# First tiles normalised ahead of their stage, and a new event order with four probability tiles in the softmax attentions

## The chip, the cores and the metric

One core of a Trainium2 chip. The metric is the device time of one execution in microseconds (us).

## What is computed

The input `x` is [4, 1024, 128] float32, that is 4096 tokens in 32 tiles of 128 tokens. Four layers each do a feed-forward part, an attention and the feed-forward part again, and each of the twelve reads a layer norm (without gain) of `x` and adds to `x`:

```python
x = x + 0.5 * _L0_ffn_ref(_layernorm(x), ...)      # FP4-quantised gated FFN, 128 -> 352 -> 128
x = x + _L0_attn_ref(_layernorm(x), ...)           # causal softmax attention, 16 heads of 8, then an 8-step scan and an FFN
x = x + 0.5 * _L0_ffn_ref(_layernorm(x), ...)
x = x + 0.5 * _L1_ffn_ref(_layernorm(x), ...)      # 8 experts, top 2
x = x + _L1_attn_ref(_layernorm(x), ...)           # softmax attention, no mask
...                                                # L1 ffn; L2: experts and a shared expert, linear attention with rope
x = x + 0.5 * _L3_ffn_ref(_layernorm(x), ...)      # 128 -> 512 -> 512 -> 512 -> 128
x = x + _L3_attn_ref(_layernorm(x), ...)           # linear attention
x = x + 0.5 * _L3_ffn_ref(_layernorm(x), ...)
```

## The kernel before

`x` stays in SBUF as `g.x` [128, 32, 128]. The program is a row of stages, each one `nc.Block` with a program per engine (PE, DVE, ACT, POOL, SP); engines meet at a block's end, and the next stage's first act on SP is to clear the semaphores of the stage before (`Stage.block`). In order: `start`, `ffn0_first`, `qkv0`, `core0` (causal), `finish0`, `ffn0_second`, `moe1_first`, `qkv1`, `core1` (no mask), `project1`, `moe1_second`, `moe2_first`, `attn2`, `moe2_second`, `ffn3_first`, `attn3`, `ffn3_second`. In the profile digits are left out of names, so that both `core` stages are "core", `moe1_first` and `moe2_first` are "moe_first", `ffn0_first` and `ffn3_first` "ffn_first".

**Front of a stage.** Most stages work in eight chunks of four tiles (CT = 4). `Front` (L129) has per chunk: `statistics` (DVE: four `bn_stats`, a small memset, four `bn_aggr`), `power` (POOL: add of epsilon, power of -0.5), `normalise` (DVE: four `tensor_scalar`), `turn` (PE transposes), `copy` (ACT). Its buffers are double. A chunk's statistics are issued a chunk or two ahead inside the stage, but the first chunk's cannot start before the stage. The expert stages (`sparse_stage`, L218) do it in four groups of eight tiles (GT = 8, L541 to L557 on DVE, L326 on POOL), write `xn` into the arena and store each group to DRAM by SP (L311).

**Ends of stages.** DVE adds the result of a chunk to `g.x`: `add` at L1548 (ffn0) and L1059 (linear attention), `summed` at L906 (ffn3), and in the expert stages for each chunk c `weighted(c, 0)` (L674) and the add at L689, as the expert rows of a chunk come back by DMA (SP, L322; four chunks at once, the next when a chunk has been added).

**Softmax cores.** `core_stage` (L1988) goes through 16 rounds, one for each batch and group of four heads. All engines follow one list of events, made by `order()` from a string, the rhythm. Per round, causal / not causal: `f` (41 / 55), a first score product of 128 queries (PE, 64 rows of the array, into one of three banks `one`), whose row maximum DVE takes; `d` (4 / 5), a difference of two key halves into a bank pair of `two`, folded by ACT's Relu, which shortens the maxima; `s` (24 / 32), half a step of second scores (two products, on both row halves of the array, into one of two bank pairs `two`), of which ACT takes the exponential (L2358) into `pr`; `w` (12 / 16), one step's product with the values (eight float32 matmuls of PE, L2337) out of `pr`; `o` (2), the output's transpose. When all maxima of a round are there, `rows`, `turn` and `split` bring them into rows of the queries, by way of DRAM (SP: L2178 store, L2183 two loads, each waited for); the round's first `s` waits for that. `ahead` counts the `f` events between the first `split` and the first `s`, and this distance holds in every later round. `pr` has two buffers: the exponential of step k waits until step k-2 has been weighed, and the k-th `w` weighs step k-1.

PE pairs matmuls: `turns` (L2258) lets a matmul of one row half follow one of the other, so that the two run side by side.

## Time and profile before

| | us |
|---|---|
| median of 3 runs | 3804.12 (3800.93 to 3805.26) |
| the profiled execution | 3801.16 |
| its span | 3799.2 |
| busy in the span: PE, DVE, ACT, POOL | 3159.1, 2525.5, 1999.8, 1127.6 |
| granted clock of TensorE, mean | 0.915 |

Lengths of stages, from the first DVE operation of each to that of the next: ffn0_first 18.6 to 181.6, qkv0 to 252.5, core0 to 687.6, finish0 to 911.0, ffn0_second to 1075.6, moe1_first to 1392.4, qkv1 to 1447.2, core1 to 2098, project1 to 2115, moe1_second to 2431, moe2_first to 2763.9, attn2 to 2851.9, moe2_second to 3182.2, ffn3_first to 3454.8, attn3 to 3525.7, ffn3_second to 3799.

Busy time is the time in which an engine had an instruction under way. Matmuls overlap on PE, so that PE counts as busy also where single matmuls follow each other with gaps between their data.

### The profile page before, as it was taken

To read this page: it belongs to the slowest core of one execution; us is meant where nothing else is said; L and a number is where in the kernel's file an instruction comes from. 1 tells how busy PE (TensorE), PEld (TensorE's weight loads), DVE (VectorE), ACT (ScalarE), POOL (GpSimd) and SP (SyncE) were. 2 spreads that over 40 slices of the span, in tenths; PEclk is the share of its full clock that TensorE was granted. 3 is DMA by queue.
4 is the path that set the end of the run, shared out by engine and by line. 5 is a ranking of instruction groups with operands and counts; after the bars stand their busy time and mean duration, and the time that the engine had idled before them with its cause. 6 is when DMAs were issued, how large, how long until landed. Compare 5 with 4: busy or idle time off the path is not lost. (4 is left out here: it accounts for less than half of the span.)

```text
span 3799.2 us, 61584 instructions
## 1 busy us (share of the span) xinstructions
PE 3159.1 (83%) x20415; PEld 1964.7 (52%) x20415; DVE 2525.5 (66%) x7054; ACT 1999.8 (53%) x2981; POOL 1127.6 (30%) x1154
## 2 busy tenths in 40 slices
PE   4659999786659967999999599687777886998899
PEld 2433333343447842222222488566656774887687
DVE  8888887575974458999995644453476345665665
ACT  1248888663214446999999144322332234664464
POOL 3454550111426631101010266246432651001000
PEclk8879999997869988999999699799988998999999
DMA  1043330000021132000000411401102113000100
GB/s 55 1 136 120 124 123 14 1 1 23 1 111 41 43 93 69 28 20 28 19 20 2 163 42 43 141 25 44 60 18 76 44 41 115 1 1 1 64 9 12
DMA packets 87166, 187.17 MB, mean 49 GB/s; under 512 B 23168, under 2 KB 41408, under 8 KB 83792
## 3 DMA queue, kind: packets, MB, share of 16 engines
q1 hardware_dynamic: 60048, 117.66, 9.2%
q0 software_dynamic: 26816, 65.58, 5.6%
q8 instruction: 178, 2.92, 0.3%
q14 instruction: 124, 1.02, 0.1%
HBM read 121.23 MB, written 61.34 MB: 48 GB/s over the span
## 5 line engine op out<-in xcount | busy, mean ns | idle before, releaser
L2358 ACT ACTIVATE core_pr<-core_two 128x1024 f32<-128x1024 f32 (+3 forms) x896 | 792.9, 936 | 73.7 <-PE core_two L2325 68.6
L2394 DVE TENSOR_REDUCE core_mx<-core_one 128x1 f32<-128x512 f32 x778 | 494.9, 685 | 44.7 <-PE core_one L2277 38.4
L2337 PE MATMUL core_ps_o<-core_pr,core_vals 128*32 128x512 f32 (+3 forms) x3584 | 437.9, 561 | 1.4 <-ACT core_oT L2369 0.9
L2277 PE MATMUL core_one<-arena,queries 64*128 64x512 bf16 (+3 forms) x1472 | 385.5, 363 | 32.3 <-PEq L62 18.4
L2325 PE MATMUL core_two<-queries,arena 64*128 64x512 bf16 (+3 forms) x1792 | 360.2, 360 | 14.5 <-ACT core_pr L2358 10.1
L2277 PEld LDWEIGHTS core_one<-arena,queries 64*128 64x128 bf16 x1472 | 112.9, 94 | 313.9 <-DVE core_mx L2394 155.8
L2211 POOL COPY core_vals<-arena 128x288 f32<-128x288 f32 x32 | 14.5, 453 | 712.6 <-PE core_ps_o L2337 712.6
L2388 DVE CUSTOM_DVE_ANT_0 core_junk<-core_one,core_over 128x512 bf16<-128x512 f32 (+4 forms) x334 | 202.6, 643 | 10.5 <-PE core_one L2277 8.8
L2325 PEld LDWEIGHTS core_two<-queries,arena 64*128 64x128 bf16 x1792 | 94.8, 94 | 206.1 <-ACT core_pr L2358 147.7
L2391 DVE CUSTOM_DVE_ANT_0 core_junk<-core_one,behind 128x128 bf16<-128x128 f32 (+1 forms) x360 | 152.1, 460 | 50.0 <-PE core_one L2277 49.8
L2364 ACT ACTIVATE core_over<-core_two 128x1024 f32<-128x1024 f32 (+4 forms) x167 | 157.7, 953 | 52.3 <-PE core_two L2300 39.1
L343 POOL DMA_INDIRECT expert_out<-arena,moe_second_dest_index x142 | 139.8, 985 | 147.5 <-ACT arena L516 127.5
L343 POOL DMA_INDIRECT expert_out<-arena,moe_first_dest_index x142 | 139.6, 983 | 147.9 <-ACT arena L516 128.8
L453 PE MATMUL moe_first_bank<-arena 128*128 x1136 | 157.5, 282 | 21.7 <-ACT arena L516 12.7
L453 PE MATMUL moe_second_bank<-arena 128*128 x1136 | 158.8, 284 | 17.3 <-ACT arena L516 9.8
L453 PEld LDWEIGHTS moe_first_bank<-arena 128*128 128x128 f32 x1136 | 140.3, 194 | 30.9 <-issue 29.4
L453 PEld LDWEIGHTS moe_second_bank<-arena 128*128 128x128 f32 x1136 | 141.5, 196 | 28.0 <-issue 27.7
L2337 PEld LDWEIGHTS core_ps_o<-core_pr,core_vals 128*32 128x32 f32 x3584 | 71.1, 108 | 131.8 <-issue 120.5
L110 DVE CAST moe_second_x_hi<-moe_second_bank 128x128 fp32r<-128x128 f32 x142 | 41.3, 291 | 143.9 <-PE moe_second_bank L426 104.5
L110 DVE CAST moe_first_x_hi<-moe_first_bank 128x128 fp32r<-128x128 f32 x142 | 41.3, 291 | 136.1 <-PE moe_first_bank L426 112.2
L516 ACT ACTIVATE arena<-moe_second_bank 128x128 f32<-128x128 f32 x142 | 39.4, 277 | 158.1 <-PE moe_second_bank L453 111.9
L516 ACT ACTIVATE arena<-moe_first_bank 128x128 f32<-128x128 f32 x142 | 39.4, 277 | 157.5 <-PE moe_first_bank L453 114.5
(577 smaller groups left out, 8090.4 us busy)
## 6 DMA issues: line engine op xcount, KB each, us to landing
arena<-expert_out SPq DMA_DIRECT2D x64, 256.0 KB, 3.6
expert_rows<-arena SPq DMA_DIRECT2D x16, 512.0 KB, 12.1
core_w_raw<-in_m_up POOLq DMA_DIRECT2D x25, 256.0 KB, 3.4
m_hi<-core_w_hi POOLq DMA_DIRECT2D x25, 256.0 KB, 2.4
m_lo<-core_w_lo POOLq DMA_DIRECT2D x25, 256.0 KB, 3.0
q_parts<-qkv_parts SPq DMA_DIRECT2D x16, 384.0 KB, 2.6
k_parts<-qkv_parts SPq DMA_DIRECT2D x16, 384.0 KB, 3.4
queries<-q_parts SPq DMA_DIRECT2D x64, 96.0 KB
```

The costliest lines, as they stand in the source:

```text
L110: return v.tensor_copy(dst.bitcast(F32R), src)
L343: p.indirect_dma_start(ys, bass.IndirectOffsetOnAxis(ap=dest[:, s:s + 1], axis=0), y[:, s % YB, :], None).then_inc(s_sc[s % YB], 16)
L453: mm = pe.matmul(psY[:, 0:P], hT[:, s % 2, j * P:(j + 1) * P], w_down[:, j * P:][:, bass.ds(at[s], P)], start=(j == 0), stop=(j == 3))
L516: a.activation(y[:, s % YB, :], psY[:, 0:P], ACT.Identity).then_inc(s_y, 1)
L2277: pe.matmul(one[bank[e]][:, 0:width], q_sb[rows, hq, pair, qt * P:(qt + 1) * P], k_sb[rows, hq, pair, kc * CW:kc * CW + width], start=True ...
L2325: mm = pe.matmul(into[:, side, off:CW], k_sb[rows, hq, pair, j * P:(j + 1) * P], q_sb[rows, hq, pair, c * CW + off:(c + 1) * CW], start=no ...
L2337: mm = pe.matmul(ps_o[h * 32:(h + 1) * 32, off:CW], vals[:, hq % 2, j, h, :], pr[:, k % 2, h // 2, h % 2, off:CW], start=(j == 0), stop=(k ...
L2358: a.activation(pr[:, k % 2, i, :, off:CW], two[spot[e] % 2][:, :, off:CW], ACT.Exp, scale=HD ** -0.5).then_inc(s_wide, 1)
L2364: a.activation(over[:, nth[e] % 2, :, 0:w], two[spot[e] % 2][:, :, 0:w], ACT.Relu).then_inc(s_wide, 1)
L2388: v.tensor_tensor_reduce(junk[:, bank[e], 0:width], scores, over[:, nth["diff", n, k, 0] % 2, side, 0:width], 1.0, -3.0e38, ALU.add, ALU.m ...
L2391: v.tensor_tensor_reduce(junk[:, bank[e], 0:width], scores, g.behind[:, CW - width:CW], 1.0, -3.0e38, ALU.add, ALU.max, at).then_inc(s_rea ...
L2394: v.tensor_reduce(at, scores, AX.X, ALU.max).then_inc(s_read, 1)
```

## The change

- A class `Head`. A stage built with `ahead=n` takes, at its end, the statistics of the first n tiles of `g.x`, once these have their last value, and normalises them into one of two buffers that outlast the stage (`g.head_xn`). The next stage's `Front` (or `sparse_stage`) takes it over: for its first chunk (group) each of `statistics`, `power` and `normalise` is only an increment of the semaphore, and `turn` reads the head's tiles. Ten stages get one: ffn0_first, finish0, moe1_first, moe2_first, moe2_second, ffn3_first and attn3 by four tiles (in the order of the work: for qkv0, ffn0_second, qkv1, attn2, ffn3_first, attn3 and ffn3_second), ffn0_second, moe1_second and attn2 by eight (for moe1_first, moe2_first and moe2_second). It adds five semaphores to each of the ten stages.
- Where it is put: ffn0, before the last `add`; sparse, statistics after the add of chunk 3, normalise after that of chunk 5; ffn3, in the last chunk at j = 2 and j = 3; linear attention, statistics before the last `cut`, normalise before the last two adds; finish0, in round BATCH at i = 4 and 6. POOL's power comes last in each POOL program.
- Softmax cores: `pr` has KEPT = 4 buffers in place of 2; the k-th `w` weighs step k-2 in place of k-1 (`lag`); both rhythms are new, with the same number of each letter; `ahead` is 13 and 8 in place of 12 and 11.
- In ffn3 the buffer `hidden1` lies in the `room` of the weights.

```diff
+class Head:
+    def __init__(self, st, g, n):
+        u = g.head_turn
+        g.head_turn = 1 - u
...
+    def statistics(self, v):
+        for k in range(self.n):
+            last = v.bn_stats(self.stats[:, k, :], flat(tile_of(self.g.x, k)))
+        last.then_inc(self.s_stats, 1)
+        v.wait_ge(self.s_stats, 1)
+        v.memset(self.dummy[:], 0.0)
+        for k in range(self.n):
+            last = v.bn_aggr(self.mv[:, k, :], self.stats[:, k, :])
+        last.then_inc(self.s_mv, 1)
+    def power(self, p):
+        p.wait_ge(self.s_mv, 1)
+        p.tensor_tensor(self.ve[:, 0:self.n], self.mv[:, 0:self.n, 1], self.g.eps[:, 0:self.n], ALU.add).then_inc(self.s_ve, 1)
+        p.wait_ge(self.s_ve, 1)
+        p.tensor_tensor(self.rstd[:, 0:self.n], self.ve[:, 0:self.n], self.g.mhalf[:, 0:self.n], ALU.pow).then_inc(self.s_rstd, 1)
+    def normalise(self, v):
+        v.wait_ge(self.s_rstd, 1)
+        for k in range(self.n):
+            last = v.tensor_scalar(self.xn[:, k, :], flat(tile_of(self.g.x, k)), self.mv[:, k, 0:1],
+                                   self.rstd[:, k:k + 1], ALU.subtract, ALU.mult)
+        last.then_inc(self.s_xn, 1)
...
     def statistics(self, v, c, u):
+        if c == 0 and self.head:
+            v.sem_inc(self.s_stats, 1)
+            v.sem_inc(self.s_mv, 1)
+            return
...
     def normalise(self, v, c, u, signal=True):
+        if c == 0 and self.head:
+            v.sem_inc(self.s_xn, 1)
+            return
...
@@ sparse_stage
+                if c == AT and head:
+                    v.wait_ge(s_sum, 2)
+                    head.statistics(v)
+                if c == AT + 2 and head:
+                    head.normalise(v)
@@ linear_stage
+            if head:
+                v.wait_ge(s_x, 2)
+                head.statistics(v)
             cut(last // 2)
             add(last - 2)
             divide(last - 1)
             divide(last)
+            if head:
+                head.normalise(v)
             add(last - 1)
             add(last)
@@ ffn0_stage
+            if head:
+                v.wait_ge(s_sum, 3)
+                head.statistics(v)
+                head.normalise(v)
             add(last)
@@ core_stage
-RHYTHMS = {True: (12, "fsffsfwffsfsffwsffdfsfwfsdffsfwsfsfwffsofswfdsofswfsffswsfffswfsffswffssffwffsdsffw"),
-           False: (11, "sfsfwfssffwffdfdfofsfswsfffswsfsffwsfdfffswsfffswfssffwffsfsfwffssfwfsfosfwsfffdswsfffswfsfdfsffwsff"
-                   "sfwfssffwf")}
+KEPT = 4
+RHYTHMS = {True: (13, 2, "fswffsffsfwffdsffwsfffssffssffsfwsffsfwwosffswfffdswoffsswsffwffssfwfffsdffswsfsfdf"),
+           False: (8, 2, "sfwffsfwffssfwfsffdofdfswsfffswfsfdffsfwsffsfwfssffwsfffswsfsffwfsfsfwfsffswffdffsfswsffsofdfswsfffs"
+                      "wsfsffwffs")}
-            steps_done, chunks_done = itertools.count(n * N2 - 1), itertools.count(2 * n - 1)
+            steps_done, chunks_done = itertools.count(n * N2 - lag), itertools.count(2 * n - 1)
-                    if step >= 2:
-                        a.wait_ge(s_weighed, step - 1)
-                    a.activation(pr[:, k % 2, i, :, off:CW], two[spot[e] % 2][:, :, off:CW], ACT.Exp, scale=HD ** -0.5).then_inc(s_wide, 1)
+                    if step >= KEPT:
+                        a.wait_ge(s_weighed, step + 1 - KEPT)
+                    a.activation(pr[:, step % KEPT, i, :, off:CW], two[spot[e] % 2][:, :, off:CW], ACT.Exp, scale=HD ** -0.5).then_inc(s_wide, 1)
```

## Rows read from the trace of the kernel before

**Rows 1.** Busy time in one round of each attention; columns in the first line.
```profile
core 0: us, PE busy (x) PEld busy (x) DVE busy (x) ACT busy (x) POOL busy (x), PEclk, DMA share, GB/s
...
425.24:450.64 25.40, 25.08 (x296) 9.03 (x290) 21.48 (x81) 22.36 (x32) 13.74 (x18) 1.00 0.41 129
...
1664.36:1703.04 38.68, 37.79 (x278) 9.43 (x276) 35.97 (x74) 36.59 (x40) 3.17 (x2) 1.00 0.08 23
```

**Rows 2.** Waits: ACT and DVE, a causal round, then a plain round.
```profile
ACT core_pr L2358 <- PE core_two L2325: 2.8, 8, 0.7
...
DVE core_junk L2391 <- PE core_one L2277: 3.0, 5, 1.0
...
ACT core_pr L2358 <- PE core_two L2325: 1.5, 6, 0.5
...
DVE core_mx L2394 <- PE core_one L2277: 2.1, 5, 0.7
```

**Rows 3.** Timeline (start, us, engine, line, operation): start of moe1_first.
```profile
1074.61 0.69 DVE L1551 SCALAR_TENSOR_TENSOR x<-ffn_second_ps_d,x 128x512 f32<-128x512 f32 x1 [9.20 <-PE ffn_second_ps_d L1654]
...
1075.62 1.64 DVE L544 BATCH_NORM_STATS2 moe_first_ln_stats<-x 128x6 f32<-128x128 f32 x8 [0.32 <-PEq L62]
...
1080.06 2.11 DVE L554 TENSOR_SCALAR arena<-x,moe_first_ln_mv,moe_first_ln_rstd 128x128 f32<-128x128 f32 x8
...
1085.46 1.11 PE L362 MATMUL moe_first_bank<-ident,arena 128*128 128x128 f32 x4 [0.52 <-DVE arena L554]
```

**Rows 4.** Timeline at the starts of qkv0, qkv1 and attn2.
```profile
185.48 0.87 DVE L1762 BATCH_NORM_STATS2 qkv_again_stats<-qkv_ln_xn 128x6 f32<-128x128 f32 x4
...
1398.47 1.12 PE L180 MATMUL qkv_ln_psT<-ident,qkv_ln_xn 128*128 128x128 f32 x4 [1.09 <-DVE qkv_ln_xn L170]
...
2769.65 2.05 PE L1124 MATMUL attn_ps_q<-attn_ln_xT,arena 128*128 128x512 f32 x2 [0.78 <-ACT attn_ln_xT L185]
```

**Rows 5.** ffn3_second: weight DMA's issue and landing (last column), first product.
```profile
3528.46 0.43 SPq L740 DMA_DIRECT2D ffn_second_f_w_lo<-f_lo  x1
...
ffn_second_f_w_lo<-f_lo SPq DMA_DIRECT2D x1, 256.0 KB, 4.8
...
3534.41 0.78 PE L121 MATMUL ffn_second_pair<-ffn_second_x_hi,ffn_second_f_w_hi 128*128 128x512 f32 x1
```

**Rows 6.** Timeline of DVE in the tail of moe1_second.
```profile
2424.70 1.14 DVE L678 SCALAR_TENSOR_TENSOR x<-arena,moe_second_weight,x 128x128 f32<-128x128 f32 x4 [0.64 <-DMA arena<-expert_out]
```

**Rows 7.** POOL's power beside a DVE operation, ffn0_second.
```profile
919.12 1.19 POOL L164 TENSOR_TENSOR ffn_second_ln_rstd<-ffn_second_ln_ve,minus_half 128x4 f32<-128x4 f32 x1
...
919.48 0.69 DVE L1348 SCALAR_TENSOR_TENSOR ffn_second_zq_v<-ffn_second_zq_v,ffn_second_zq_magic 128x512 f32<-128x512 f32 x1
```

**Rows 8.** Timeline of PE in a plain round.
```profile
1674.05 0.38 PE L2277 MATMUL core_one<-arena,queries 64*128 64x512 bf16 x2
...
1674.48 0.38 PE L2277 MATMUL core_one<-arena,queries 64*128 64x512 bf16 x1
...
1674.79 1.07 PE L2337 MATMUL core_ps_o<-core_pr,core_vals 128*32 128x512 f32 x8
```

**Rows 9.** Timeline of PE: value products of the causal attention, alone and adjacent.
```profile
437.76 0.64 PE L2337 MATMUL core_ps_o<-core_pr,core_vals 128*32 128x256 f32 x8
...
439.81 0.43 PE L2337 MATMUL core_ps_o<-core_pr,core_vals 128*32 128x128 f32 x8
...
684.55 1.01 PE L2337 MATMUL core_ps_o<-core_pr,core_vals 128*32 128x256 f32 x16
```

**Rows 10.** SP's DMA issues in a plain round, and landing of L2178, whole run.
```profile
1669.20 0.32 SPq L2178 DMA_DIRECT2D maxima<-core_nm  x1
...
1670.66 1.48 SPq L2183 DMA_DIRECT2D queries<-maxima  x2
...
1676.67 2.28 SPq L1800 DMA_DIRECT2D queries<-q_parts  x6
...
DMA to landing us min/median/max: 1.4/1.5/3.1
```

More of the change, by code:

```diff
@@ L160, in power @@
     def power(self, p, c, u):
+        if isinstance(c, int) and c == 0 and self.head:
+            p.sem_inc(self.s_ve, 1)
+            p.sem_inc(self.s_rstd, 1)
+            return
         p.wait_ge(self.s_mv, c + 1)
@@ L179, in turn @@
         for k in range(CT):
-            last = pe.transpose(self.psT[:, k * P:(k + 1) * P], (source or self.xn)[:, u, k, :], self.g.ident[:])
+            last = pe.transpose(self.psT[:, k * P:(k + 1) * P], (source[:, u] if source else self.tiles(c))[:, k, :], self.g.ident[:])
         last.then_inc(self.s_turned, 1)
@@ L351, in _ @@
                 scatter(s)
-                for ahead in itertools.islice(rest, min(MORE, max(0, s + R + 1 - min(FIRST + MORE * s, s + R)))):
-                    gather(ahead)
+                for n in itertools.islice(rest, min(MORE, max(0, s + R + 1 - min(FIRST + MORE * s, s + R)))):
+                    gather(n)
+            if head:
+                head.power(p)
         @block.tensor
@@ L705, in ffn3_stage @@
     f = Front(st, g)
+    head = Head(st, g, ahead) if ahead else None
     s = st.sb("silu", [P, 2, CW])
@@ L757, in _ @@
             over_chunks(p, body)
+            if head:
+                head.power(p)
         @block.tensor
@@ L916, in body @@
                         hidden(c + 1, j)
+                    if j == 2 and last and head:
+                        v.wait_ge(s_summed, 2)
+                        head.statistics(v)
+                    if j == 3 and last and head:
+                        head.normalise(v)
                     if j == 1 and c:
@@ L1115, in _ @@
                     f.power(p, c + 2, u)
+            if head:
+                head.power(p)
         @block.tensor
@@ L1509, in normalise @@
                     return
+                if c == 0 and f.head:
+                    v.sem_inc(f.s_xn, 1)
+                    return
                 v.wait_ge(f.s_rstd, c + 1)
@@ L1588, in _ @@
                 h_inverses(c + 1)
+            if head:
+                v.wait_ge(s_sum, 3)
+                head.statistics(v)
+                head.normalise(v)
             add(last)
@@ L1628, in _ @@
                 x_divide(c + 4)
+            if head:
+                head.power(p)
         @block.tensor
@@ L1884, in once @@
                     return
-                v.wait_ge(f.s_rstd, c + 1)
-                if c >= 2:
-                    v.wait_ge(f.s_xn, c - 1)
-                for k in range(CT):
-                    end = v.tensor_scalar(f.xn[:, u, k, :], flat(tile_of(g.x, c * CT + k)), f.mv[:, u, k, 0:1],
-                                          f.rstd[:, u, k:k + 1], ALU.subtract, ALU.mult)
-                end.then_inc(s_once, 1)
-                v.wait_ge(s_once, c + 1)
-                again.statistics(v, [f.xn[:, u, k, :] for k in range(CT)], c, u)
+                if c == 0 and f.head:
+                    v.sem_inc(s_once, 1)
+                else:
+                    v.wait_ge(f.s_rstd, c + 1)
+                    if c >= 2:
+                        v.wait_ge(f.s_xn, c - 1)
+                    for k in range(CT):
+                        end = v.tensor_scalar(f.xn[:, u, k, :], flat(tile_of(g.x, c * CT + k)), f.mv[:, u, k, 0:1],
+                                              f.rstd[:, u, k:k + 1], ALU.subtract, ALU.mult)
+                    end.then_inc(s_once, 1)
+                    v.wait_ge(s_once, c + 1)
+                again.statistics(v, [f.tiles(c)[:, k, :] for k in range(CT)], c, u)
             def twice(c):
@@ L1898, in twice @@
                     v.wait_ge(f.s_turned, c + 1)
-                    again.apply(v, [f.xn[:, u, k, :] for k in range(CT)], [xn2[:, u, k, :] for k in range(CT)], c, u).then_inc(f.s_xn, 1)
+                    again.apply(v, [f.tiles(c)[:, k, :] for k in range(CT)], [xn2[:, u, k, :] for k in range(CT)], c, u).then_inc(f.s_xn, 1)
             statistics(0)
@@ L2089, in put_out @@
                 products += 1
-        ahead, rhythm = RHYTHMS[causal]
+        ahead, lag, rhythm = RHYTHMS[causal]
         while ("split", 0, 0, 0) not in events:
@@ L2115, in order @@
                 normalise()
-        weigh(N * N2 - 1)
+        for step in range(N * N2 - lag, N * N2):
+            weigh(step)
         put_out(2 * N - 1)
@@ L2544, in finish0_stage @@
     rounds = range(-1, BATCH + 2)
+    head = Head(st, g, ahead) if ahead else None
     with st.block() as block:
@@ L2558, in _ @@
                         n1.power(p, at(b + 1, a) - 1, a)
+            if head:
+                head.power(p)
         @block.tensor
@@ L2831, in _ @@
                         hidden(b - 1)
+                    if b == BATCH and i == 4 and head:
+                        v.wait_ge(s_x, 2)
+                        head.statistics(v)
+                    if b == BATCH and i == 6 and head:
+                        head.normalise(v)
                     if i == 3 and ahead:
```

84 lines of the change are left out of this document (61 added, 23 removed).

## Prediction

> **What bounds the kernel now.** I read the stage table first: the two softmax cores are 435 and 651 us of 3799, and fifteen other stages share the rest, so a change at stage borders acts ten times by a little, a change of a round 32 times. Next, one round of each core in the windows view [rows 1]. A causal round takes 25.40 us and PE is busy for 25.08 of it; a plain round takes 38.68, with PE 37.79, ACT 36.59 and DVE 35.97. The reader is to see that PE is the bound in the causal rounds, and that in the plain ones all three are close. The waits view says the same from the other side [rows 2]: ACT waits 2.8 us for PE in a causal round and 1.5 in a plain one, DVE 3.0 and 2.1. Nobody is seen to wait for the probability buffers themselves. Last, the timelines at the borders. In an expert stage's front DVE needs 4.4 us from the stage's start (1075.62) until it can normalise the first group (1080.06), and PE gets the second group at 1085.46 after a short wait for DVE [rows 3]: DVE's chain sets the front's pace.
>
> **Borders, the gain.** No work is added or taken away: statistics, power and normalising of the first tiles move ahead of the border.
> Eight tiles for an expert stage: removed from its front are 1.64 us of statistics with about 0.6 of aggregation, and 2.11 of normalising [rows 3], 4.35 together. New order on DVE: statistics of groups 1 and 2 (2 x 2.24 = 4.5), then half of normalise(1), 1.05, so that PE gets the second group 5.6 us after the start where it was 9.84 (1085.46 less 1075.62): 4.2 us, three times, 12.6.
> Four tiles, from the same kinds of rows at half size (statistics 1.2, normalising 1.1, and the wait for POOL between). qkv0 starts its second norm at 185.48, 3.8 us in [rows 4]; with the head only statistics(1) stand before it, 1.2: 2.6. ffn0_second does the same work behind a memset: 2.5. qkv1's second transpose, which PE has before its first product, starts at 1398.47, 6.1 us in, and waits for DVE [rows 4]; now two statistics, power already under way, and normalise(1): 3.9, gain 2.2. In attn2 the first product starts 5.75 us in (2769.65) [rows 4]; statistics, power and normalising leave its chain, some 3.7, of which ACT's table load at the start keeps about 0.2: 3.5, and the same in attn3. In the ffn3 stages the front would gain 3, but the first product also waits for four weight loads. The last is issued at 3528.46 and lands 4.8 us later, 3533.3, and the product starts at 3534.41 [rows 5]: at most 1.1 to gain; SP has five more semaphores to clear before it issues, so 1.0 in ffn3_second, and in ffn3_first, where SP starts later still, 0.3. Four-tile heads: 2.6 + 2.5 + 2.2 + 3.5 + 3.5 + 1.0 + 0.3 = 15.6. Gross 28.2.
>
> **Borders, the cost.** In ffn0 DVE idles 9.20 us before the last add [rows 3]; eight tiles need 2.24 + 1.9 on POOL + 2.11 = 6.3, and the add queued behind does not feel it. Without that idle stretch it would cost all of it. finish0, ffn3_first and attn3 have DVE idle in the same way: 0. attn2's eight-tile normalise is 2.1 against a gap of some 1.9: 0.2. The tails of the expert stages have no such gap. DVE waits there for returning rows only for moments (0.64 us before chunk 5) [rows 6], no DMA is held up (all loads are released before the head's first instruction), and DVE works through the chunks one after the other. Eight tiles: 2.24 less 0.64, then 2.11, less what later waits absorb: 3.3 (moe1_second). Four tiles: 1.2 + 1.1 = 2.3, less these waits: 0.3 to 1.5 at each of three borders, 3.0 in all. Cost 6.5, net gain **21.7**. Bounds: 12 if the tails pay everything and the ffn3 stages gain nothing, 26 if the tails pay half.
>
> At the tails POOL's power runs beside DVE adds with two SBUF inputs. The row shows a power of 1.19 us (919.12) and such an operation at 919.48 inside it, which takes 0.69, its usual time [rows 7]; so I charge nothing. The Trainium skill says otherwise (SBUF — State Buffer, "SBUF: two separate sides"): the port pair shared by VectorE and GpSimd is an exclusive lock held for a whole instruction. By that rule each of five tails would hold DVE for up to a power, 1.2 to 1.9 us, some 6 in all, and the net gain would be 15.
>
> **Causal core.** PE is the bound, so what counts is PE's time per round. PE pairs matmuls of opposite row halves: the pair at 1674.05 takes 0.38, as long as the single one at 1674.48 [rows 8]; a single one between pairs wastes about 0.11. Between `w`, `o` and `w` I count half slots (f 1, s 2, d 4): an odd number wastes one. Before: 7 odd stretches of 14. After: 5 of 14, so 0.2 less. Each switch to a `w` also costs: after the single f at 1674.48 it starts 0.31 later, not 0.22 [rows 8], and a `w` has its own tail; two adjacent ones of 256 and 128 columns take 1.01 where 0.64 and 0.43 are 1.07 [rows 9]. So a `w` next to a `w` or `o` saves some 0.15. The new causal rhythm has three such places, made possible by the deeper `pr`; the old had none: 0.45. Together 0.65, taken as 0.7 with some gain from fewer waits, in 15.5 rounds: **10.9**. Bounds per round: -2.8, when ACT waits for nothing any more [rows 2]; +0.7, one of ACT's longest waits more, since a run of six `s` without `w` now stands in the round.
>
> **Plain core.** The same count gives 15 odd stretches after, 13 before, +0.2, and no adjacent `w`. At its `w` events the new order is mostly as far from the exponential it needs as the old one (two `s` before, and two now). Four buffers relieve a wait that the trace does not show. What is left is order alone: half a microsecond of shorter waits less 0.2, I take 0.25 per round, **3.9** in all. Bounds: -2.1, DVE's waits for PE gone [rows 2]; +0.9, the odd stretches and one long wait.
>
> The smaller `ahead` shortens the lead of the maxima's way through DRAM: the first load is issued at 1670.66 after a store at 1669.20; 1.48 for two issues and 1.4 to land give 1673.5, while SP sees the old round's last `s` done at 1676.67 [rows 10], 3.1 us of spare. Three `f` fewer take 3/55 of 38.68, 2.1. So 1.0 stays and costs nothing. The end of each core gets one more `w` behind the last exponentials, up to 0.5 each, set against an earlier start of core1's `s`.
>
> **Sum.** 21.7 + 10.9 + 3.9 = 36.5 off the profiled execution's 3801.2: 3764.7. The median of the runs is 2.9 above that execution: **3768**.
>
> **Rivals.**
> - Rhythms worth nothing (0.20): PE's pairing is lost to semaphore timing. Against it: the counts. 3804.1 - 21.7 = 3782.
> - Rhythms worth much (0.13): the orders remove half of the waits, 1.4 and 1.0 per round, 37 us, and the heads 21.7: 3745. For it: waits of 2 to 3 us per round on two engines; against it: PE's busy time leaves 0.3 and 0.9.
> - Heads absorbed (0.06): the first product of a stage has another wait behind the removed one, as in ffn3. Then the borders give 7 and the rhythms 10: 3787.
> - Slower (0.05): the maxima's way decides in the plain core. If each of its two legs takes 3.1 us, the longest landing seen [rows 10], in place of 1.4, the spare of 1.0 becomes a wait of 2.4 in 15 rounds, 36 us; with the heads' gain and nothing from the causal core, 3818. It decides from a lead of less than a microsecond on.
>
> **Numbers.** The forecast case has 0.56 with its own range 3756 to 3780. The range for 8 in 10 is 3744 to 3790: it leaves out the slower case, half of the absorbed one and the far ends of the second and third. A measurement can tell 0.2%, 7.6 us. Faster by more: 0.56 + 0.20 + 0.13, and 0.03 of the absorbed case, 0.92; slower by more: 0.04; within: 0.04.
>
> **What the profile would show.** Period of the causal rounds 24.7 us (25.40), of the plain ones 38.4 (38.68). In an expert front the second group's transposes 5.6 us after the stage's first DVE operation; ffn0's last add with about 3 us idle before it; the tail of moe1_second longer by 3.3. It is wrong if the plain period rises, if PE's first `s` of a round waits for "queries<-maxima", if DVE operations in the tails stretch beside POOL's power, or if fronts start early and the end of the stage does not move.

## The result

The changed kernel takes 3758.9 us (median of 4, 3755.9 to 3762.5) against 3802.5 for the kernel before, timed beside it; the ratio on record is 0.9898 (0.9886 to 0.9909), 35 to 43 us faster, where the two medians by themselves are 43.6 us apart (0.9885), just outside that interval. The forecast was 3768 with a range of 3744 to 3790. The profiled execution took 3759.6 us, its span is 3757.8.

The page of the changed kernel, its span and part 1:

```profile
span 3757.8 us, 61674 instructions
## 1 busy us (share of the span) xinstructions
PE 3150.6 (84%) x20415; PEld 1975.6 (53%) x20415; DVE 2525.3 (67%) x7057; ACT 1992.2 (53%) x2981; POOL 1128.5 (30%) x1154
```

DVE, ACT and POOL do the same work as before, to within 8 us of busy time; PE is busy for 8.5 us less. All of the change is in when things are done.

**One round of each core**, the windows view of the changed kernel, answering to [rows 1]:

```profile
core 0: us, PE busy (x) PEld busy (x) DVE busy (x) ACT busy (x) POOL busy (x), PEclk, DMA share, GB/s
469.38:493.97 24.59, 24.33 (x293) 9.50 (x293) 22.42 (x82) 22.11 (x31) 13.77 (x18) 1.00 0.43 133
1753.73:1791.73 38.00, 37.77 (x280) 9.76 (x278) 35.49 (x73) 36.33 (x40) 3.17 (x2) 1.00 0.09 24
```

A causal round fell from 25.40 to 24.57 us in most rounds (24.48 in the last four), a plain one from 38.68 to 38.00, to a hundredth the same in 14 rounds. Over 15 rounds that is 12.5 and 10.2 us. The waits view of the same rounds, answering to [rows 2] (total us, times, longest):

```profile
ACT core_pr L2473 <- PE core_two L2440: 1.8, 4, 0.7
...
DVE core_junk L2506 <- PE core_one L2392: 1.7, 5, 0.7
...
ACT core_pr L2473 <- PE core_two L2440: 0.9, 4, 0.3
...
DVE core_junk L2503 <- PE core_one L2392: 1.3, 2, 0.8
DVE core_mx L2509 <- PE core_one L2392: 0.6, 2, 0.4
```

The first two are the causal round's, where they were 2.8 and 3.0; the others the plain round's, where ACT's was 1.5 and DVE's 2.1, which is 1.9 in two lines now. All but the last fell clearly, but in a round whose length is set by PE they would fall anyway when PE gets quicker. What came first is not in this view.

**DVE beside POOL.** DVE is busy for 22.42 us of the causal round where it was 21.48. Nearly all of the difference is one small cast, by which the maxima's `split` makes a bf16 part. The timeline of POOL and DVE in the round above, and of DVE in a later one:

```profile
472.62 1.27 POOL L2341 TENSOR_TENSOR core_w_lo<-core_w_raw,core_w_hi 128x512 fp32r<-128x512 f32 x1
472.84 1.13 DVE L2522 CAST core_nm<-core_left 32x128 bf16<-32x128 f32 x1
...
571.12 0.21 DVE L2522 CAST core_nm<-core_left 32x128 bf16<-32x128 f32 x1
```

In the eight rounds in which POOL's operation (part of its work on weights) starts just before the cast, the cast takes 1.11 to 1.13 us and ends 0.08 us behind POOL's; in others it takes 0.21. In steady rounds of the old order the two don't meet, and it takes 0.21 throughout. The new order put it where POOL is at work. When POOL's work on the weights is over, in the last four rounds, the period is 24.48 us, and the step that has become shorter is an `f` that waits for DVE behind the `split`: this costs some 0.09 us a round.

**A front and a tail.** The timeline (start, us, engine, line, operation) from the end of ffn0_second into moe1_first, answering to [rows 3]:

```profile
1048.03 1.63 DVE L147 BATCH_NORM_STATS2 ffn_second_head_stats<-x 128x6 f32<-128x128 f32 x8
...
1052.37 2.14 DVE L164 TENSOR_SCALAR head_xn<-x,head_mv,head_rstd 128x128 f32<-128x128 f32 x8 [2.03 <-POOL head_rstd L159]
...
1057.15 0.69 DVE L1655 SCALAR_TENSOR_TENSOR x<-ffn_second_ps_d,x 128x512 f32<-128x512 f32 x1 [2.64 <-PE ffn_second_ps_d L1764]
1058.35 1.65 DVE L620 BATCH_NORM_STATS2 moe_first_ln_stats<-x 128x6 f32<-128x128 f32 x8 [0.50 <-PEq L62]
...
1060.22 1.07 PE L434 MATMUL moe_first_bank<-ident,head_xn 128*128 128x128 f32 x8 [3.11 <-DVEq L629]
...
1063.93 1.12 PE L434 MATMUL moe_first_bank<-ident,arena 128*128 128x128 f32 x4 [0.52 <-DVE arena L633]
```

The head of eight tiles lies whole in DVE's idle stretch: of 9.20 us ahead of the last add 2.64 are left, and the add still waits for PE. In the next stage the second group is transposed 5.58 us after the stage's first DVE operation (1063.93 less 1058.35), where it was 9.84.

The same view of DVE and POOL in the tail of moe1_second, answering to [rows 6] and [rows 7]:

```profile
2391.00 1.14 DVE L757 SCALAR_TENSOR_TENSOR x<-arena,moe_second_weight,x 128x128 f32<-128x128 f32 x4 [0.25 <-DMA arena<-expert_out]
...
2392.66 1.64 DVE L147 BATCH_NORM_STATS2 moe_second_head_stats<-x 128x6 f32<-128x128 f32 x8
...
2394.90 1.11 DVE L757 SCALAR_TENSOR_TENSOR x<-arena,moe_second_weight,x 128x128 f32<-128x128 f32 x4
2395.92 0.68 DVE L768 TENSOR_TENSOR x<-x,arena 128x512 f32<-128x512 f32 x1
2396.53 1.13 DVE L757 SCALAR_TENSOR_TENSOR x<-arena,moe_second_weight,x 128x128 f32<-128x128 f32 x4
...
2398.18 2.13 DVE L164 TENSOR_SCALAR head_xn<-x,head_mv,head_rstd 128x128 f32<-128x128 f32 x8
...
2395.35 1.67 POOL L159 TENSOR_TENSOR head_rstd<-head_ve,minus_half 128x8 f32<-128x8 f32 x1
```

Here there is no idle stretch to lie in: DVE has no wait from 2391.00 to the end, and each head operation pushes the rest back. POOL's power (2395.35 to 2397.02) runs beside 2395.92 and 2396.53, which take the usual 0.68 and 1.13.

**By stages.** The traces show each meeting of the engines at a block's end. From one to the next, in us, with the kernel of the cores alone (below) as a second measure of what a stage takes without a head. It ran on another chip, on which the expert stages are shorter (last section), so they are compared by their tails only:

| stage | before | after | cores alone |
|---|---|---|---|
| qkv0 | 70.85 | 68.66 | 71.11 |
| core0 | 435.42 | 421.18 | 424.00 |
| ffn0_second | 165.49 | 161.71 | 165.48 |
| qkv1 | 54.77 | 51.72 | 54.64 |
| core1 | 651.18 | 641.28 | 640.89 |
| moe1_second | 315.86 | 320.04 | |
| moe2_first | 332.81 | 323.45 | |
| attn2 | 88.02 | 83.32 | 86.38 |
| attn3 | 70.67 | 67.11 | 70.50 |
| ffn0_first | 163.95 | 168.56 | 165.26 |
| ffn3_second | 273.71 | 277.30 | 273.63 |

The stages left out changed by -3.1 (moe1_first) to +1.1 us (project1). The last two rows are a warning. ffn0_first came out 4.6 us longer though its head lies in a gap. Four fifths of that is there before the head: its last chunk's `hq_magic` (L1346 before, L1446 after) starts 3.60 us later. The first stage does not come near the changed lines until its last chunk. moe2_first is a warning the other way: it is 9.4 us shorter, of which its front and its tail explain 2 (4.07 gained, 2.0 paid, see below). With its head it took 329 to 336 us in the four `cut` kernels on two other chips, and of the two kernels on a third chip the one with heads took 295.2, the one without 293.7. So one profile of a stage can be off by some 4 us, and of an expert stage by 7, and the gain of the heads is not read from these rows but from the kernels below.

### The profile page after: what moved, and what is told of

Same layout as the page of the kernel before. It is cut to its first block and busy times, and to the rows that moved or that the text cites. A ratio compares the mean times of both kernels' runs of the same rounds, so it can differ in the third digit from the quotient of the medians.

```text
span 3757.8 us, 61674 instructions
## 1 busy us (share of the span) xinstructions
PE 3150.6 (84%) x20415; PEld 1975.6 (53%) x20415; DVE 2525.3 (67%) x7057; ACT 1992.2 (53%) x2981; POOL 1128.5 (30%) x1154
## 5 line engine op out<-in xcount | busy, mean ns | idle before, releaser
L2392 PE MATMUL core_one<-arena,queries 64*128 64x512 bf16 (+3 forms) x1472 | 375.8, 363 | 28.2 <-PEq L62 18.4
L2440 PE MATMUL core_two<-queries,arena 64*128 64x512 bf16 (+3 forms) x1792 | 342.4, 360 | 9.4 <-ACT core_pr L2473 6.8
L2503 DVE CUSTOM_DVE_ANT_0 core_junk<-core_one,core_over 128x512 bf16<-128x512 f32 (+4 forms) x334 | 202.2, 644 | 25.7 <-PE core_one L2392 21.0
L525 PE MATMUL moe_first_bank<-arena 128*128 x1136 | 158.0, 283 | 19.3 <-ACT arena L588 10.9
## 6 DMA issues: line engine op xcount, KB each, us to landing
expert_rows<-arena SPq DMA_DIRECT2D x13, 512.0 KB, 12.6
```

Source lines behind the costliest of these rows:

```text
L525: mm = pe.matmul(psY[:, 0:P], hT[:, s % 2, j * P:(j + 1) * P], w_down[:, j * P:][:, bass.ds(at[s], P)], start=(j == 0), stop=(j == 3))
L2392: pe.matmul(one[bank[e]][:, 0:width], q_sb[rows, hq, pair, qt * P:(qt + 1) * P], k_sb[rows, hq, pair, kc * CW:kc * CW + width], start=True ...
L2440: mm = pe.matmul(into[:, side, off:CW], k_sb[rows, hq, pair, j * P:(j + 1) * P], q_sb[rows, hq, pair, c * CW + off:(c + 1) * CW], start=no ...
L2503: v.tensor_tensor_reduce(junk[:, bank[e], 0:width], scores, over[:, nth["diff", n, k, 0] % 2, side, 0:width], 1.0, -3.0e38, ALU.add, ALU.m ...
```

## Experiments

The kernels of the first two parts up to `lag_two` ran 4 to 10 times, the others once each, so that from these only periods and positions within the profile are read. Periods are those of the rounds in steady state (from one `rows` reduction of DVE to the next), which within a run repeat to 0.02 us over most rounds (but for `new_order_lag_one`); where a chip's clock or the expert stages differ, that does not touch them: the kernel before's 25.40 and 38.67 came back on both chips.

### The parts alone

```diff
 heads_only:   KEPT = 2, old strings, lag 1, ahead 12 and 11
 cores_only:   no stage has ahead=
```

Heads only. 

> The changed kernel with the old rhythms and two probability buffers, so that only the heads are left of the change. The profile after shows both cores 24.1 us shorter than before, which leaves some 17 to 20 of the 43.6 us for the borders. If the borders give what the forecast says (21.7), this kernel takes 3781 us and the periods of the rounds are those of before, 25.40 and 38.68. If the heads are absorbed by other waits (rival), it takes 3795 or more, and the changed kernel's gain has to come from the rounds and their ends.

Measured: 3675.8 us where the kernel before takes 3695.7, ratio 0.9948 (0.9931 to 0.9965), 13 to 26 us faster; periods 25.40 and 38.67.

Cores only. 

> The changed kernel without any head; only the softmax cores are new. Periods 24.57 and 38.00 as in the changed kernel, so 15 rounds of each give 0.83 x 15 + 0.68 x 15 = 22.7 us and the two cores' lengths 24: 3779 us. If heads and cores add up, the two gains (this one and that of the heads alone) sum to 43.6. A rival: the cores' gain hangs on state left by the heads (clock, SBUF places), then the periods here differ from 24.57 and 38.00 by more than 0.1.

Measured: 3673.2 us, ratio 0.9942 (0.992 to 0.9964), 13 to 30 us faster; periods 24.57 and 38.00 (37.99 in most rounds). The two gains, 19 and 21, add up to the 39 of the whole change within their intervals. As far as these intervals can tell, heads and cores don't touch each other, so from here on several questions ride in one kernel, each read in its own stage.

### The buffers and the distance

```diff
 four_buffers:  KEPT = 4, old strings, lag 1
 lag_two:       KEPT = 4, old strings, lag 2
 new_order_lag_one:  KEPT = 4, new strings, lag 1
```

Four buffers. 

> The changed kernel with the old rhythms and the old distance (the k-th weighing takes step k-1), but four probability buffers. My theory: the depth alone does nothing, since nobody was seen to wait for the buffers: periods 25.40 and 38.68, total as with the heads alone. Rival: the depth itself lets ACT run ahead and takes its waits: periods fall towards 24.57 and 38.00.

Measured: 25.40 and 38.67, ratio 0.9957 (0.9945 to 0.9969), that of the heads alone. The depth by itself is worth nothing.

Distance of two. 

> As the one with four buffers and the old rhythms, but the k-th weighing takes step k-2. My theory (the order of the letters makes the gain in the causal core, through pairing and adjacent value products): causal period stays at 25.4 within 0.2, plain at 38.68 within 0.2, since PE's list has the same odd stretches and the same switches. Rival (PE waited at each weighing for the exponential, and the larger distance removes that): most of the 0.83 and 0.68 appears here, periods near 24.7 and 38.1.

Measured: 25.29 and 39.33. The distance by itself makes the plain core worse by 0.65 a round, outside what I gave it. The waits view of a plain round, first of the kernel with lag two, then of that with four buffers:

```profile
PE core_one L2459 <- DVE core_mx L2508: 0.9, 2, 0.6
```

```profile
PE core_one L2459 <- DVE core_mx L2508: 0.2, 1, 0.2
```

L2459 is the output's transpose, `o`. Its place among the letters is the same in both. What moved is ACT's copy of the output that it reads: with a distance of two it stands one `w` later. In the kernel with lag two one `o` waits 0.64 us; that copy ends at 1790.95 and the last maximum at 1790.97, and `o` starts at 1791.10. With four buffers alone the same copy ended 1.8 us before its `o`. The view puts the wait down to the maxima, which came last; how much is the copy's was not separated.

New order, distance of one. 

> The new rhythms with four buffers, but the k-th weighing takes step k-1 as before. If the order of the letters is all, the periods are 24.57 and 38.00. If order and distance belong together, a weighing right behind its second scores waits for the exponential (0.9 us) or for the one before: at the adjacent pair of the causal rhythm and at each place with a single s ahead of a w. I expect the causal period at 25.2 or more and the plain one at 38.7 or more.

Measured: 33.1 (up to 34.5 in some rounds) and 57.6 (59.0 in every third plain round), 4133 us in all. Far worse than I expected. The waits view of PE in one plain round:

```profile
PE core_ps_o L2451 <- ACT core_pr L2472: 18.9, 15, 1.6
```

15 of 16 weighings wait for their exponential, 1.3 us each on the average. So buffers, distance and order are one design. By itself the depth gives nothing, the distance 0.11 in the causal core against 0.66 lost in the plain one, and the order harm. That the distance of two needs the deeper `pr` is read from the kernel's waits: no run has it with fewer than four.

### Is it PE's own row of work, or its waits?

PE is busy for 98% of a round in either kernel, and yet one is shorter. Busy time can't tell a short row of matmuls from one with short waits in it. The Trainium skill says so too (Perfetto Trace Analysis, "Identifying the Most-Contended Engine"): the occupancy of matmuls is no measure of how near PE is to its limit; the table below agrees, with about 2 us of waits in a round that counts as 98% busy. So I made the others quick: from a core's second round on the exponential takes one bank of the pair, and in the two `cut` pairs the maxima take half of the scores as well (in the causal core only those that have no mask). The values of the attention are then not the reference's.

```diff
-a.activation(pr[:, step % KEPT, i, :, off:CW], two[spot[e] % 2][:, :, off:CW], ACT.Exp, ...
+some = 2 if n == 0 else 1
+a.activation(pr[:, step % KEPT, i, 0:some, off:CW], two[spot[e] % 2][:, 0:some, off:CW], ACT.Exp, ...
```

```diff
 cut_old_plain, cut_new_plain (in the causal pair: causal, and no mask):
+some = 1 if n and not causal else 2
...
+if n and not causal:
+    width //= 2
 scores = one[bank[e]][:, 0:width]
```

ACT cut, old order. 

> Old rhythms, old distance, four buffers; from the second round on each exponential is taken of half its columns only (one bank of the pair), so ACT has some 40% less to do in the cores and the attention's values are not the reference's. It shows what of a period is PE's own row of work. If PE's order alone sets both periods, they stay within 0.2 of 25.40 and 38.68. If PE's short gaps in front of second scores come from waiting for ACT to empty a bank pair (which PE's busy time hides), the plain period falls, by up to 0.7 or more, to 38.0 or below; the causal one, where ACT has 3 us of spare, falls by less than 0.3.

ACT cut, new order. 

> The same cut of the exponentials, with the new rhythms and the distance of two. Theory one, pairing and adjacency: the differences between old and new stay as they are without the cut, 0.83 in the causal and 0.68 in the plain core. Theory two, shorter waits for ACT: the difference in the plain core shrinks to under 0.3, since the old order is freed of its waits too; in the causal core most of the 0.83 stays, because there I hold PE's own row of work for the bound.

ACT and DVE cut in the plain core; a causal string with one letter moved. New order: 

> Two tests in one, one for each core. Plain core, new order: from the second round on the exponential takes half of its columns, and each row maximum is taken of half of the scores, so that neither ACT nor DVE can hold PE up and the period is PE's own row of work (the values are not the reference's). With the cut of ACT alone the period was 37.34 here and 38.02 with the old order. Theory one (PE's own row differs): the difference of 0.68 stays. Theory two (PE waits for DVE's maxima in its three banks): it falls below 0.2. Causal core, nothing cut: the new order with one weighing moved behind the next f (ssfwfff becomes ssffwff). By my count of pairs a round of the new order takes PE 25920 columns, the old one 28480, this one 24704: 1216 less, at 2.4 GHz 0.51 us. If the number of columns sets the causal period, it falls from 24.57 to 24.1; if the count is not what decides, it stays within 0.15.

Old order: 

> The same cut in the plain core with the old order and the distance of one; see the other: its period less that of the new order is 0.68 by theory one, under 0.2 by theory two. Causal core, nothing cut: the new order with another weighing moved behind the next f (ffwffss becomes fffwfss), which raises the count of columns from 25920 to 26944: 0.43 us more, 25.0, if the columns set the period; within 0.15 of 24.57 if not.

ACT and DVE cut in the causal core; the plain core with another ahead; no head in front of the ffn3 stages. Old order: 

> Three tests, each read in its own rows. Causal core, old order and distance: from the second round on half of each exponential and of the maxima that have no mask is left out (the values are not the reference's), so ACT and DVE can't hold PE up; with ACT alone cut the period was 25.26. Compare with the new order under the same cut: if PE's own row of work differs (pairs, adjacent weighings), the difference stays above 0.6; if it was DVE's maxima, it falls below 0.3. Plain core, nothing cut: the old order with ahead 8 in place of 11: if the smaller ahead is what relieved DVE, the period falls from 38.67 to about 38.3; if the letters do it, it stays within 0.15, or rises where the phase does not fit. Borders: no head at the end of moe2_second. If its tail costs more than it gives, moe2_second ends 1.5 to 2.5 us sooner after its last matmul (25.2 to 26.6 us with the head, 23.8 without), and ffn3_first's ninth matmul starts only 0.2 to 0.6 later (9.19 in place of 8.6 to 9.0).

New order: 

> Causal core: the same cut with the new order; with ACT alone cut it was 24.42. See the other. Plain core, nothing cut: the new order with ahead 7 in place of 8. 10 gave 39.54; if a phase that fits is a matter of a single f, 7 is worse too, 38.3 or more. Borders: no head for either ffn3 stage: both ninth matmuls start at 9.15 to 9.2 us. In moe1_second the head's first eight statistics are taken twice, the first time into a tile that nobody reads (1.64 us more on DVE). If DVE is the bound of that tail, its length from the last matmul on grows from 26 to 27 us by 1.6 to 28 or more; if the returning rows or POOL's power set it, by less than 0.6.

Measured, in us per round:

| | plain old | plain new | difference | causal old | causal new | difference |
|---|---|---|---|---|---|---|
| nothing cut | 38.68 | 38.00 | 0.68 | 25.40 | 24.57 | 0.83 |
| ACT cut | 38.02 | 37.34 | 0.68 | 25.26 | 24.42 | 0.84 |
| ACT and DVE cut | 36.77 | 36.45 | 0.32 | 24.52 | 23.83 | 0.69 |

The windows view of one plain round with both cut, old order and then new:

```profile
1748.94:1785.71 36.77, 36.47 (x278) 9.37 (x277) 22.41 (x73) 23.72 (x40) 3.17 (x2) 1.00 0.09 25
```

```profile
1749.51:1785.96 36.45, 36.20 (x284) 9.43 (x276) 22.24 (x74) 23.72 (x40) 3.18 (x2) 1.00 0.09 25
```

And of one causal round with both cut, old and new:

```profile
468.82:493.34 24.52, 24.09 (x294) 9.45 (x290) 17.93 (x81) 15.17 (x31) 13.77 (x18) 1.00 0.43 132
```

```profile
460.61:484.44 23.83, 23.43 (x292) 9.49 (x292) 18.95 (x81) 15.54 (x31) 13.77 (x18) 1.00 0.44 137
```

With DVE and ACT at 60 to 65% of the plain round, a round is still 36.5 us long: that is about what PE's own row takes, and 2 us of the 38.7 were waiting that its busy time hides. In the plain core 0.32 of the 0.68 is PE's own row; the other 0.36 went when DVE was cut as well, and not with ACT alone, so I put it down to waiting for the maxima (no run cut DVE alone). The wait for ACT (0.65 a round) is there in the old order and the new alike. Neither of my two theories is right for the plain core; each has half.

In the causal core 0.69 of the 0.83 stays, and that is the least that PE's own row gives. In the new order the `split` is still held up beside POOL, now its L2530 for 1.37 us in place of 0.28, and one `f` waits 0.34 us for DVE (`arena`, L2536). In the last three rounds, with POOL done, neither is there and the period is 23.31; the old order stays at 24.52 to the end, with a wait of 0.29 of its own before an `o`. So PE's own row is shorter by 0.9 to 1.2 us (24.52 less 23.31, with and without that 0.29), and the uncut kernel keeps 0.83 of it.

**Is it the columns?** A count of pairs gives PE 28480 columns a round for the old causal order and 25920 for the new, 1.07 us at 2.4 GHz, and 38400 and 38912 for the plain ones. The causal strings with one letter moved:

| causal string | columns by count | expected from the count | measured |
|---|---|---|---|
| new | 25920 | | 24.57 |
| ssfwfff to ssffwff | 24704 | 24.1 | 24.93 |
| ffwffss to fffwfss | 26944 | 25.0 | 24.68 |

Old to new, the count's 1.07 fits the 0.9 to 1.2 of the causal row above. But for single letters it fails: the string with fewer columns is the slower one. 0.3 of its 0.36 is one wait that the move opened, before an `f`:

```profile
PE core_one L2391 <- DVE core_mx L2511: 0.3, 1, 0.3
```

Without it the period would still not fall by the 0.5 that the count gives, and the string with 0.43 us more of columns lost 0.11, with no wait in the view. In the plain core the count has the wrong sign, with the others cut too. So it doesn't set the period by itself. A weighing moved by one `f` cost 0.1 to 0.4 us whichever way the pairs went.

**Where in PE's row?** From one matmul's start to the next, summed by letter over one round (`t` is the turn of the maxima), in us:

| | `w` | `s` | `d` | `f` | `o`, `t` | round |
|---|---|---|---|---|---|---|
| causal before | 9.53 | 6.97 | 2.22 | 5.18 | 1.49 | 25.40 |
| causal after | 9.18 | 6.75 | 1.92 | 5.22 | 1.52 | 24.58 |
| causal old, both cut | 9.48 | 7.55 | 1.81 | 4.20 | 1.48 | 24.52 |
| causal new, both cut | 9.23 | 6.60 | 1.76 | 4.72 | 1.52 | 23.82 |
| plain before | 15.97 | 9.89 | 2.38 | 8.91 | 1.53 | 38.68 |
| plain after | 15.97 | 8.78 | 2.51 | 9.13 | 1.60 | 38.00 |
| plain old, both cut | 15.97 | 8.82 | 2.16 | 8.31 | 1.52 | 36.77 |
| plain new, both cut | 15.97 | 8.63 | 2.57 | 7.76 | 1.52 | 36.45 |

In the causal core `w` gives 0.35 of the 0.83, `s` and `d` 0.52. A weighing of 512, 384, 256 or 128 columns takes 1.00, 0.79, 0.57 or 0.36 to the next start. Of the three adjacent places one saves 0.11 (a 256 before a `w`, 0.46), one 0.03 (a 128 before an `o`, 0.33) and one nothing (a 512 before an `o`, 1.00): 0.14. The other 0.2 is at two weighings of the old order with a longer gap behind them (0.70 and 0.46, for a 256 and a 128). In the plain core, with nothing cut, `s` falls by 1.1 and the others give back 0.4. With both cut its gain is in `f` (0.55) and `s` (0.19), and `d` gives back 0.4. So a gain moves between letters as waits come and go, and no single kind of step holds it.

### Adjacency and the phase

```diff
-causal: ..sffsfwwosffswfffdswoffssw..     plain: ahead 8
+causal: ..sffsfwswffoswfffdswffossw..     plain: ahead 10
```

> The changed kernel with the three adjacent places of the causal rhythm taken apart (wwos becomes wswffo, woffs becomes wffos; number of letters and evenness of the stretches as they were), and with ahead 10 in place of 8 in the plain core. Adjacency theory: the causal period rises by 3 x 0.15 = 0.45, to 25.0. Rival: adjacency is worth nothing beside the even stretches, then it stays within 0.1 of 24.57. For the plain core: ahead is only a phase, 38.00 within 0.15; if the smaller lead is part of the gain, it rises by more.

Measured: 27.65 and 39.54, both by far worse than either theory has it. The waits view of PE, the causal round and then the plain one:

```profile
PE core_one L2391 <- DVE arena L2529: 1.9, 2, 1.0
PE core_ps_o L2451 <- ACT core_oT L2483: 0.5, 1, 0.5
...
PE core_one L2391 <- DVE core_left L2519: 1.4, 1, 1.4
```

L2529 is DVE's normalising of the output that sits in one of the three banks, L2519 the maxima's `split`. Moving the `o` by two letters put its bank's reader behind other work of DVE, and the first products wait. So this run can't price adjacency: it opened a wait of another kind. What the plain core shows is the phase: two more `f` between the split and the first `s` cost 1.5 us a round. The later runs say the same: the new plain order with ahead 7 takes 39.74, the old one with ahead 8 takes 40.70, where each takes 38.0 and 38.7 with its own.

### The tails and the ffn3 fronts

In one kernel the head of moe1_second took its first eight statistics twice:

```diff
     def statistics(self, v):
+        if self.spare is not None:
+            for k in range(self.n):
+                v.bn_stats(self.spare[:, k, :], flat(tile_of(self.g.x, k)))
         for k in range(self.n):
```

The timeline of DVE in that kernel:

```profile
2406.97 1.64 DVE L149 BATCH_NORM_STATS2 moe_second_head_spare<-x 128x6 f32<-128x128 f32 x8
2408.52 1.63 DVE L151 BATCH_NORM_STATS2 moe_second_head_stats<-x 128x6 f32<-128x128 f32 x8
...
2414.03 2.13 DVE L168 TENSOR_SCALAR head_xn<-x,head_mv,head_rstd 128x128 f32<-128x128 f32 x8
```

From the stage's last matmul to its end, in us, over all profiles taken:

| tail of | without head | with head | cost |
|---|---|---|---|
| moe1_first (4 tiles) | 22.74, 22.98 | 23.4 to 25.5, mean 24.3 of 12 | 1.4 |
| moe1_second (8) | 22.82, 22.95 | 25.7 to 27.2, mean 26.4 of 11 | 3.5 |
| moe1_second, statistics twice | | 28.59 | 5.7 |
| moe2_first (4) | 23.30, 23.63 | 24.9 to 26.4, mean 25.5 of 12 | 2.0 |
| moe2_second (4) | 22.97 to 24.04, mean 23.7 of 4 | 24.6 to 26.6, mean 25.6 of 10 | 1.9 |

The doubled work of 1.64 us made the tail 2.2 longer than the mean and 1.4 longer than the longest other: as far as one profile tells, DVE is the bound of this tail. The returning rows' waits absorb a fifth of eight tiles (3.5 paid of 2.24 + 2.11), and of four tiles 0.3 to 0.9 of 2.3.

The ffn3 fronts: the ninth matmul starts at 9.19 in all four profiles without a head and at 8.2 to 9.0 (mean 8.66 of 10) with one in ffn3_first; at 9.10 to 9.15 and at 7.9 to 9.2 (mean 8.4 of 11) in ffn3_second. That 0.5 and 0.7 is what is gained, and then the clock takes over. The windows view of the first 30 us of ffn3_second, 6 us each, the changed kernel and then the one with heads alone (the last three numbers are the granted clock, the DMA share and GB/s):

```profile
3480.80:3486.80 6.00, 1.74 (x8) 1.13 (x8) 3.48 (x15) 0.68 (x2) 1.88 (x2) 0.85 0.54 167
3486.80:3492.80 6.00, 2.90 (x6) 1.83 (x6) 0.10 (x1) 2.48 (x3) 0.00 (x0) 0.50 0.98 374
3492.80:3498.80 6.00, 3.73 (x8) 2.52 (x9) 3.31 (x6) 0.69 (x1) 0.00 (x0) 0.50 0.97 401
3498.80:3504.80 6.00, 4.44 (x11) 2.95 (x11) 2.21 (x4) 0.69 (x1) 0.00 (x0) 0.50 0.06 24
3504.80:3510.80 6.00, 5.40 (x22) 4.09 (x21) 3.76 (x7) 2.66 (x3) 0.00 (x0) 0.95 0.00 0
```

```profile
3404.50:3410.50 6.00, 1.74 (x8) 1.13 (x8) 3.48 (x15) 0.61 (x2) 1.88 (x2) 0.88 0.49 157
3410.50:3416.50 6.00, 2.90 (x6) 1.82 (x6) 0.17 (x1) 2.55 (x3) 0.00 (x0) 0.56 1.00 376
3416.50:3422.50 6.00, 3.33 (x12) 2.10 (x12) 3.58 (x6) 1.11 (x2) 0.00 (x0) 1.00 0.97 403
3422.50:3428.50 6.00, 4.24 (x17) 3.17 (x18) 4.23 (x8) 2.23 (x3) 0.00 (x0) 1.00 0.08 30
```

The work of the stage is the same. In one the clock is back at full (2.4 GHz) some 12 us in, in the other it stays at half (1.2 GHz) until 24 us in, and the stage is 4 us longer (277.30 and 273.37). With a head 4 of 11 profiles of this stage are of the long kind, without one none of 3; in ffn3_first both kinds occur with a head and without. Whether the head's early transposes, with an idle PE behind them while the weights land, make the long kind likelier is left open: a few profiles can't tell.

A version without the head at the end of moe2_second gains 1.9 there and loses 0.5 in the next front. That is 0.04% of the time, less than a total can show, and no such version was timed by itself.

## Why the prediction was right, and where not

The forecast was 36.5 off the profiled execution; that execution's span fell by 41.4: the cores gave 24.1 where I had 14.8, all the rest 17.3 where I had 21.7. So two errors of opposite sign stand behind the 9 us. Another 3.6 of them is the step from one execution to the median: I added 2.9, and the changed kernel's median lies 0.7 below its profiled execution.

- **Fronts, forecast 28.2.** The expert fronts gain 4.07 at the 17th matmul after the engines' meeting (10.08 to 6.01 us in), 12.2 for three; I had 12.6. The stages qkv0, ffn0_second, qkv1, attn2 and attn3 with their heads are shorter by 2.4, 3.4, 2.3, 5.2 and 3.5 (means of 12 profiles less means of two); I had 2.6, 2.5, 2.2, 3.5 and 3.5. The ffn3 fronts gain 0.5 and 0.7 where I had 0.3 and 1.0. Sum 30, with a clock's play of some us in the last stages' terms.
- **Tails, forecast 6.5.** 8.8 measured. The eight tiles cost 3.5 (3.3 forecast); the four-tile heads 1.4, 2.0 and 1.9, 5.3 in place of 3.0. The mis-sized step is "less these waits: 0.3 to 1.5 at each of three borders": each was to cost 0.3 to 1.5, 3.0 in all, and each cost 1.4 to 2.0, since the waits took only 0.3 to 0.9 off 2.3. ffn0's idle stretch hid a whole head, as forecast: 2.64 left where I had some 3.
- **Net 21.7** against 19.2 (13 to 26) with the heads alone.
- **POOL's power beside DVE.** Charged at nothing, and DVE's operations beside it kept their 0.68 and 1.13. What the Trainium skill says (SBUF — State Buffer, "SBUF: two separate sides"), an exclusive lock of the shared port pair for a whole instruction, would have held one of them for up to 1.67; beside the power this trace does not show it. Elsewhere it does: the cast of the `split` in the new causal order takes 1.13 in place of 0.21, to the end of POOL's operation of 1.27. I looked for such a hold only where the heads are, and the new order has it in the core, at some 0.09 a round.
- **Causal core, forecast 0.7 a round and 10.9.** 0.83 a round, 12.5, and at least 0.69 of it in PE's own row, as I said. The terms came out otherwise. "So a `w` next to a `w` or `o` saves some 0.15", at three places 0.45, was mis-sized: the three save 0.14 together. The odd stretches, 0.2, stand against 0.52 in `s` and `d`; the count of pairs behind them fits old to new, and fails for a letter moved by one place. Another 0.2 behind two weighings I had not seen at all. So that the sum of two terms came so near is in part luck, and which neighbours make a step cheap was not found.
- **Plain core, forecast 0.25 a round and 3.9.** 0.68 and 10.2: this is the term that was mis-sized most, 6.3 of the 9 us by which the median lies under the forecast. Two things failed. "The same count gives 15 odd stretches after, 13 before, +0.2": PE's own row got 0.32 shorter. And "half a microsecond of shorter waits" came out at 0.36, as far as the cuts show for DVE's maxima.
- **Lead of the maxima.** Held: no first `s` waits for the load, with ahead 8 in the new order. But "ahead" was no free slack either: 7 and 10 each cost 1.5 us or more a round.
- **Four buffers.** "Relieve a wait that the trace does not show": right, 25.40 and 38.67 with four buffers alone; they are what the order stands on.

The rival "rhythms worth much" (3745) had half of the waits gone; the result lies between it and the forecast. The slower rival did not come.

## What to carry to other kernels

- Work moved ahead of a border is free where the engine that does it is idle in the tail, and costs most of its length where that engine ends the stage (3.5 of 4.35 us, 1.4 to 2.0 of 2.3); look at the last idle stretch of that engine, not at its share of busy time.
- When an engine is "busy" for 98% of a loop and reordering still shortens it, cut the other engines' work to half and look again: the period that is left is close to the engine's own row, and the rest is waiting that busy time hides. Look for the waits that are left before you call it so.
- A hand-made order in which several engines share a few banks is tuned as a whole: its distance, its phase and each letter. A single letter or phase changed cost 0.1 to 3 us a round here, the distance up to 20, so a new order is priced by running it.
- A new order on one engine moves the others too: see what now runs side by side. Here a cast of 0.21 us came to stand beside POOL's work and takes 1.13.

## What the runs showed of the hardware

- A small DVE cast from SBUF to SBUF (32x128 to bf16) waits for the end of a POOL operation that began before it: 1.13 us in place of 0.21, ending 0.08 us behind POOL's, in eight rounds of the changed kernel; in a `cut` kernel a DVE `tensor_tensor` in the same place takes 1.37 in place of 0.28. Beside POOL's power of 8 elements a partition, DVE's adds with two SBUF inputs are not held.
- The same kernel before took 3803 us on one chip and 3696 on another. Nearly all of it is in the four expert stages, which were 106 us shorter in the kernel with the cores alone on the second chip (moe2_second 301 us, and 330 on the first); what the kernels share of the cores, qkv and ffn0_second agreed to 3 us. Each run was compared with the kernel before on its own chip.
- TensorE's granted clock in the front of an ffn3 stage rises from 0.5 to 1.0 either some 12 us in or some 24 us in, in the same kernel and the same work, and that is worth 4 us of a stage: as much as any head of this change.
- Two orders of the same matmuls on opposite row halves differ by 0.69 to 1.2 us in 24 with ACT and DVE mostly out of the way. Counting what pairs up gives 1.07 there, and in the plain core 0.2 us in the wrong direction (0.32 shorter).
